# Splitting the first weight load in two, and making the first FFN weights inside the output projection

## The chip, the cores and the metric

The kernel runs on all 8 cores of one Trainium2 chip. Every core runs the same program on its own rows; two cores share a batch entry. The metric is the device time of the slowest core in microseconds, lower is better. Engines: PE (TensorE, with PEld for its weight loads), DVE (VectorE), ACT (ScalarE), POOL (GpSimd) and SP (SyncE). DMAs are issued from the instruction queues of POOL and SP.

## The reference

One transformer layer on x of shape (4, 2048, 2048):

```
q, k, v = x Wq^T, x Wk^T, x Wv^T
mem     = sum over 4 memories of softmax weight * (elu1(q) M_m) / (elu1(q) n_m)
local   = causal attention, 16 heads of 128
x1      = layernorm(x + (g*mem + (1-g)*local) Wo^T)
up      = relu(quant8(x1) ternary(Wup)^T)^2          # Wup: 4096 x 2048
out     = layernorm(x1 + quant8(up) ternary(Wdown)^T)
ternary(w) = clip(round(w / s), -1, 1) * s,   s = mean |w|
```

The ternary weights are found on the chip: a comparison of each weight with +threshold and -threshold.

## The kernel before, in words

Each core takes one batch entry, computes q for all of its 2048 tokens (stage A1), k, v and attention head pair by head pair (A2), and from then on works on its own 1024 tokens: memory retrieval (B0, B1), transposes (B2), output projection with residual (B3), quantisation with the first columns of the FFN's up product (C1), the rest of the up product (C2), then the down product and the second layernorm (C3 to C5).

The order is written out by hand. Each engine has one list of instructions, which it works through strictly in the order of the calls that emitted them; `k.emit(engine, fn, waits, inc)` puts one in, with waits on semaphores ahead of it. A DMA is issued from the list of POOL (`gpsimd`) or SP (`sync`), and its waits hold back everything behind it in that list. `k.ch(sem)` waits until the last DMA on that semaphore has landed.

**Stage A1** (L315). x (64 DMAs in four batches, a batch issued when the one before has landed), the small `mntb` and Wq (`wqb`, one DMA of 2048 x 2048 at L273) are loaded with a cast from f32 to bf16, all on POOL's queue and on the semaphore `gld`. The first group of 16 matmuls (oc = 0, lc = 0, dc = 0 to 15) waits for all of Wq.

**Stage B3** (L942 to L1010). Loop over ht = 0 to 3 (512 output columns each) and ss = 0 to 7 (128 tokens each). For each ht, POOL issues four DMAs into `wos[ht % 2]` (L942), after the matmuls of ht - 2 that read this buffer. For each (ht, ss): SP loads the residual `xos` (L955, two buffers), DVE casts it to `xob` (L963), PE does 16 matmuls (L970, of which the first waits for `wos`) and one more that adds `xob` (L976), ACT evacuates into `x2` (L982) and sums squares (L988), DVE finds minimum and maximum (L992, L996), and for ht = 3 four small reductions (L1001 to L1010). DVE's cast for a pair stands in its list ahead of that pair's reductions and behind those of the pair before.

**Between B3 and C1.** After the loop come `emit_wfs_dma(0)`, `emit_tern_up(0)`, `emit_wfs_dma(1)`, `emit_tern_up(1)` and `emit_wfs_dma(2)`. `emit_wfs_dma(it)` (L1028) loads 256 columns of Wup into the single staging tile `wfs`, half 0 from POOL's list, half 1 from SP's; each half waits until the ternary step of `it - 1` has read it. `emit_tern_up(it)` makes `wub[it % 2]` on DVE with two instructions a half (L1045, L1050). Then come 17 small operations on `sr8`, `sc3`, `ncol`, `f1col` and `cq1` (L1063 to L1097, one square root on ACT), and the loop of C1, which for each ss quantises (ACT L1133, L1138; DVE L1144, L1148), transposes (PE L1157, DVE L1163) and does the up products of it = 0 and 1 (PE L1109).

**Places in SBUF** (bytes of a partition). `lsT`, which B3's matmuls read to their end, is at 98304 to 131072; `wub1` is at 98304, so its ternary step waits for `b3_last`, the last matmul of B3. `wfs` is at 73728, `wub0` at 90112. 65536 to 73728 is free in B3 to C2 but for the tile `tnbg`, which nothing writes.

Of the kernel before, what the change touches and what calls it, by code (L numbers as in the profile page):

```python
# [9 lines left out]
BF16 = mybir.dt.bfloat16  # L10
I32 = mybir.dt.int32
ALU = mybir.AluOpType
# [4 lines left out]
D = 2048  # L17
# [3 lines left out]
NCK = 16  # L21
# [110 lines left out]
def build_program(dbg=False):  # L132
# [4 lines left out]
    wqT = dt("wqT", [D, D], F32, kind="ExternalInput")  # L137
# [5 lines left out]
    wupT = dt("wupT", [D, DI], F32, kind="ExternalInput")  # L143
# [25 lines left out]
    with root:  # L169
        k = K()  # L170
# [5 lines left out]
        gld = mksem("gld")  # L176
        sld = mksem("sld")
        sst = mksem("sst")
        tmm = mksem("tmm")
        vve = mksem("vve")  # L180
# [5 lines left out]
        s_up = mksem("s_up")  # L186
        s_dn = [mksem(f"s_dn{i}") for i in range(2)]
        s_xo = [mksem(f"s_xo{i}") for i in range(2)]
        s_sw = [mksem(f"s_sw{i}") for i in range(2)]
        gcc = mksem("gcc")  # L190
        sdbg = mksem("sdbg")

        ov = Overlay(nc)
# [20 lines left out]
        thrup = P("thrup", 128, 1, F32)  # L214
# [17 lines left out]
        def bank_w(b):  # L232
            return [bank_guard[b]] if bank_guard[b] is not None else []
# [5 lines left out]
        wqb = ov.tensor("wqb", [128, NCK * D], BF16, 0, 1)  # L239
# [5 lines left out]
        xchunk_ld = []  # L245
        for lc in range(4):
            for dc in range(NCK):
# [3 lines left out]
                    waits=k.ch(gld) if dc == 0 else (), inc=gld, inc_k=16)  # L251
            xchunk_ld.append(gld.n)
            k.chend(gld)
        for dst, src in ((biasb, biasc), (idb, identb), (onecb, onescb),
# [7 lines left out]
            waits=k.ch(sld), inc=sld, inc_k=16)  # L262
# [4 lines left out]
            waits=k.ch(gld), inc=gld, inc_k=16)  # L267
        k.chend(gld)
        k.emit("sync", lambda sy: sy.dma_start(gb[0:1, 0:1], gate.ap()),
               waits=k.ch(sld), inc=sld, inc_k=16)  # L270
        k.chend(sld)
        consts_ld = sld.n
        k.emit("gpsimd", lambda g: g.dma_start(  # L273
            wqb[:].rearrange("p (c w) -> p c w", w=D),
            wqT.ap().rearrange("(c p) w -> p c w", p=128)),
            waits=k.ch(gld), inc=gld, inc_k=16)
        wq_ld = gld.n
        k.chend(gld)
# [31 lines left out]
        for oc in range(NCK):  # L310
            for lc in range(4):
                bank = lc
                wts = [(gld, max(wq_ld, xchunk_ld[lc]))] + bank_w(bank)
                for dc in range(NCK):
                    k.emit("tensor", lambda t, oc=oc, lc=lc, dc=dc, bank=bank: t.matmul(  # L315
                        ps[bank][:, 0:CH],
                        wqb[:, dc * D + oc * 128: dc * D + (oc + 1) * 128],
                        xTb[:, dc * S + lc * CH: dc * S + (lc + 1) * CH],
                        start=(dc == 0), stop=(dc == NCK - 1)),
                        waits=wts if dc == 0 else (),  # L320
                        inc=tmm if dc == NCK - 1 else None)
                mmv = tmm.n
                if lc < 2:
                    k.emit("vector", lambda v, oc=oc, lc=lc, bank=bank: v.tensor_copy(
                        qT[:, oc * OWN + lc * CH: oc * OWN + (lc + 1) * CH],
                        ps[bank][:, 0:CH]),
                        waits=[(tmm, mmv), (vve, vve.n)], inc=vve)
                    bank_guard[bank] = (vve, vve.n)
                else:
                    par = lc - 2  # L330
                    k.emit("vector", lambda v, bank=bank, par=par: v.tensor_copy(
                        qPscr[:, par * CH:(par + 1) * CH], ps[bank][:, 0:CH]),
                        waits=[(tmm, mmv), (vve, sigch["v"])], inc=vve)
                    qcp = vve.n
                    bank_guard[bank] = (vve, qcp)
                    k.emit("scalar", lambda s, par=par: s.activation(
                        scrA1[:, par * CH:(par + 1) * CH],
                        qPscr[:, par * CH:(par + 1) * CH], AF.Relu,
                        scale=-1.0),
                        waits=[(vve, qcp), (sse, sigch["exp"])], inc=sse)  # L340
                    k.emit("scalar", lambda s, par=par: s.activation(
                        scrA2[:, par * CH:(par + 1) * CH],
                        scrA1[:, par * CH:(par + 1) * CH], AF.Exp,
                        scale=-1.0), waits=[(sse, sse.n)], inc=sse)
                    sigch["exp"] = sse.n
                    k.emit("vector", lambda v, par=par: v.scalar_tensor_tensor(
                        scrA1[:, par * CH:(par + 1) * CH],
                        qPscr[:, par * CH:(par + 1) * CH],
                        0.0, scrA2[:, par * CH:(par + 1) * CH],
                        ALU.max, ALU.add),  # L350
                        waits=[(sse, sigch["exp"]), (vve, vve.n)], inc=vve)
                    k.emit("vector", lambda v, oc=oc, par=par: v.reduce_sum(
                        sbarP[:, par * NCK + oc: par * NCK + oc + 1],
                        scrA1[:, par * CH:(par + 1) * CH], AX.X),
                        waits=[(vve, vve.n)], inc=vve)
                    sigch["v"] = vve.n
# [15 lines left out]
               waits=k.ch(sld), inc=sld, inc_k=16)  # L372
# [5 lines left out]
               waits=[(sld, consts_ld)], inc=sse)  # L378
        gsig = sse.n
        wts = [(sse, gsig)] + bank_w(2)  # L380
# [4 lines left out]
               waits=[(tmm, tmm.n)], inc=vve)  # L385
# [51 lines left out]
        for hp in range(8):  # L437
# [4 lines left out]
                waits=[(tmm, kw_t)] + k.ch(s_kv), inc=s_kv, inc_k=16)  # L442
# [6 lines left out]
                waits=[(tmm, vw_t)] + k.ch(s_kv), inc=s_kv, inc_k=16)  # L449
            vld = s_kv.n  # L450
            k.chend(s_kv)
            for hip in range(2):
                for st in range(4):
                    bank = (hip * 4 + st) % 2
                    wts = [(s_kv, kld), (gld, wq_ld)] + bank_w(bank)
                    for dc in range(NCK):
# [5 lines left out]
                            waits=wts if dc == 0 else (),  # L462
# [393 lines left out]
        for ss in range(8):  # L856
            for oc in range(NCK):
# [26 lines left out]
        sr8 = ov.tensor("sr8", [128, 48], F32, 0, 11)  # L884
        wfs = ov.tensor("wfs", [128, NCK * 256], F32, 6, 8, at=73728)
        wub = [ov.tensor("wub0", [128, NCK * 256], BF16, 6, 8, at=90112),
               ov.tensor("wub1", [128, NCK * 256], BF16, 6, 8, at=98304)]
        tnb = ov.tensor("tnb", [128, 2048], BF16, 6, 10, at=172032)
        xqT = ov.tensor("xqT", [128, 8 * D], BF16, 7, 8, at=106496)
        xqtile = ov.tensor("xqtile", [128, D], BF16, 7, 8)  # L890
# [14 lines left out]
        rqtile = ov.tensor("rqtile", [128, 2048], BF16, 9, 10)  # L905

        xob = [ov.tensor(f"xob{i}", [128, CH], BF16, 6, 6) for i in range(2)]
        tnbg = ov.tensor("tnbg", [128, 2048], BF16, 6, 6, at=65536)
        mng = ov.tensor("mng", [128, 32], F32, 6, 8)
        mxg = ov.tensor("mxg", [128, 32], F32, 6, 8)  # L910
        cq1 = ov.tensor("cq1", [128, 16], F32, 6, 8)
# [21 lines left out]
        def g_emit(fn, waits=()):  # L933
            k.emit("gpsimd", fn, waits=[(gcc, last_g[0])] + list(waits),
                   inc=gcc)
            last_g[0] = gcc.n
            return gcc.n

        for ht in range(4):
            buf = ht % 2  # L940
# [12 lines left out]
            for ss in range(8):  # L953
# [46 lines left out]
                if ht == 3:  # L1000
# [10 lines left out]
                        sc3[:, ss:ss + 1], mxg[:, ss * 4:(ss + 1) * 4],  # L1011
                        AX.X, ALU.max))
            wo_t[buf] = tmm.n
        b3_last = tmm.n
        b3_sse = last_s[0]

        up_ld = {}
        tern_half = {}
        up_t = [0, 0]
        tern_v = {}  # L1020

        def emit_wfs_dma(it):
            lds = []
            for dh in range(2):
                sem = s_up if dh == 0 else s_sw[0]
                qeng = "gpsimd" if dh == 0 else "sync"
                w0 = [tern_half[(it - 1, dh)]] if it >= 1 else []
                k.emit(qeng, lambda g, it=it, dh=dh: g.dma_start(  # L1028
                    wfs[:, dh * 2048:(dh + 1) * 2048].rearrange(
                        "p (c w) -> p c w", w=256),  # L1030
                    wupT.ap()[dh * 1024:(dh + 1) * 1024,
                              it * 256:(it + 1) * 256].rearrange(
                        "(c p) w -> p c w", p=128)),
                    waits=w0 + k.ch(sem), inc=sem, inc_k=16)
                lds.append((sem, sem.n))
                k.chend(sem)
            up_ld[it] = lds

        def emit_tern_up(it, eng="vector", extra=()):
            buf = it % 2  # L1040
            em = v_emit if eng == "vector" else g_emit
            sem = vve if eng == "vector" else gcc
            tb = tnb if eng == "vector" else tnbg
            for dh in range(2):
                em(lambda v, dh=dh, tb=tb: v.tensor_scalar(  # L1045
                    tb[:, 0:2048], wfs[:, dh * 2048:(dh + 1) * 2048], -1.0,
                    thrup[:, 0:1], ALU.mult, ALU.is_ge),
                    waits=[up_ld[it][dh], (tmm, up_t[buf]),
                           (vve, sw_v)] + list(extra))
                tv = em(lambda v, dh=dh, buf=buf, tb=tb: v.scalar_tensor_tensor(  # L1050
                    wub[buf][:, dh * 2048:(dh + 1) * 2048],
                    wfs[:, dh * 2048:(dh + 1) * 2048], thrup[:, 0:1],
                    tb[:, 0:2048], ALU.is_ge, ALU.subtract))
                tern_half[(it, dh)] = (sem, tv)
            tern_v[it] = (sem, tv)

        emit_wfs_dma(0)
        emit_tern_up(0)
        emit_wfs_dma(1)
        emit_tern_up(1, extra=[(tmm, b3_last)])  # L1060
        emit_wfs_dma(2)

        v_emit(lambda v: v.tensor_single_scalar(  # L1063
            sr8[:, 8:16], sr8[:, 0:8], 1.0 / D, ALU.mult))
# [468 lines left out]
```

How the kernel before makes its waits and increments, by code:

```python
        def g(e, fn=fn, wl=wl, inc=inc, inc_k=inc_k):  # L64
            for (h, v) in wl:
                e.wait_ge(h, v)
            r = fn(e)
            if inc is not None:
                r.then_inc(inc.h, inc_k)
```

## Time and profile before

| what | us |
|---|---|
| median of 3 runs | 3064.46 (3057.01 to 3067.91) |
| the profiled execution's own time | 3062.41 |
| its span on the slowest core (core 3) | 3060.9 |
| spans of the 8 cores | 3029.0 to 3060.9 |
| PE busy | 2268.7 (74%) |
| DVE busy | 1134.9 (37%) |
| ACT busy | 713.9 (23%) |
| PE waits for Wq at the start | 139.9 |
| stage B3, first to last matmul | 2000.5 to 2129.5 |
| stage C1, first transpose to the next ternary step | 2166.0 to 2325.6 |

Times inside the profile count from the start of the span. The span is the slowest core's, and the own time of the same execution is 1.5 us longer.

### The profile page before, as it was taken

The page shows a single profiled execution, that of the slowest core. Times are in us where ns is not written, and L with a number is a line of the kernel's source. Part 1 is how long each engine was busy: PE and PEld are TensorE (multiplying, and loading weights), DVE is VectorE, ACT ScalarE, POOL GpSimd, SP SyncE. Part 2 cuts the span into 40 slices and gives each one's busy share as a digit, 9 for nine tenths or more (in the row PEclk, how much of TensorE's full clock was granted, in tenths as well). Part 3 has the DMA queues.
Part 4 walks back from the last instruction along what each step waited for, and adds up shares of the span by engine and source line. Part 5 has one row for each costly group of instructions (what it writes and reads, how often), then busy time and mean ns, then how long its engine had stood idle before and what let it go on. Part 6 is the DMA issues. An engine that isn't in the chain of part 4 may idle for free.

```text
span 3060.9 us, 37676 instructions; the slowest of 8 cores (3029.0 to 3060.9 us)
## 1 busy us (share of the span) xinstructions
PE 2268.7 (74%) x14858; PEld 1452.9 (47%) x14858; DVE 1134.9 (37%) x1393; ACT 713.9 (23%) x1232; POOL 143.5 (5%) x166
## 2 busy tenths in 40 slices
PE   0199799898988988960799999587347992455883
PEld 0044353452543534510788888233225882344773
DVE  0043303324143243245111111535335765655544
ACT  0021123323323223233011111022232222341221
POOL 4000000000000000001000100000000000000000
PEclk9999899999999999975899999599557996677997
DMA  8700142433343333223676580174102442102422
GB/s 107 114 1 1 37 67 83 83 96 96 69 110 73 79 91 95 63 69 38 73 91 76 67 98 4 18 128 108 50 0 83 150 126 83 55 1 89 129 86 110
DMA packets 190002, 229.53 MB, mean 75 GB/s; under 512 B 10499, under 2 KB 157956, under 8 KB 188804
## 3 DMA queue, kind: packets, MB, share of 16 engines
q0 software_dynamic: 129568, 109.08, 23.1%
q1 hardware_dynamic: 59108, 109.66, 11.6%
q10 hardware_dynamic: 1152, 8.39, 0.7%
q8 instruction: 120, 1.97, 0.3%
q14 instruction: 54, 0.44, 0.1%
HBM read 294.23 MB, written 8.39 MB: 99 GB/s over the span
## 4 chain that ended last, share of the span: by engine, by line
PE 65%; DVE 15%; DMA 6%; another core or an unknown queue 5%; issue 3%; ACT 3%; DVEq 2%; POOL 0%; ACTq 0%; POOLq 0%; SPq 0%
PE ps_all L758 15%; PE ps_all L477 8%; PE ps_all L457 7%; PE ps_all L1109 7%; PE ps_all L315 7%; PE ps_all L1304 5%; PE ps_all L526 4%; PE ps_all L521 3%; PE ps_all L544 2%; PE ps_all L970 2%; DVE wdb L1267 2%; DMA wfd<-wdnT 2%; PE ps_all L420 1%; DMA membuf<-mem 1%
## 5 line engine op out<-in xcount | busy, mean ns | idle before, releaser
L758 PE MATMUL ps_all<-membuf,sigT 128*128 128x256 bf16 x4096 | 448.6, 273 | 41.8 <-DMA membuf<-mem 41.8
L758 PEld LDWEIGHTS ps_all<-membuf,sigT 128*128 128x128 bf16 x4096 | 401.4, 98 | 88.8 <-issue 41.8
L315 PE MATMUL ps_all<-xTb,wqb 128*128 128x512 bf16 x1024 | 223.3, 382 | 139.9 <-DMA wqb<-wqT 139.9
L1304 PE MATMUL ps_all<-wdb,rtq 128*128 128x256 bf16 x2048 | 255.9, 293 | 92.2 <-DVE wdb L1267 53.6
L1304 PEld LDWEIGHTS ps_all<-wdb,rtq 128*128 128x128 bf16 x2048 | 213.6, 105 | 134.4 <-issue 95.9
L1109 PE MATMUL ps_all<-wub,xqT 128*128 128x256 bf16 x2048 | 256.0, 292 | 23.0 <-DVE wub L1050 9.6
L1109 PEld LDWEIGHTS ps_all<-wub,xqT 128*128 128x128 bf16 x2048 | 212.1, 104 | 65.5 <-issue 29.5
L477 PE MATMUL ps_all<-vw,xTb 128*128 128x256 bf16 x2048 | 229.9, 276 | 12.4 <-DVE lsT L429 12.4
L457 PE MATMUL ps_all<-xTb,kw 128*128 128x512 bf16 x1024 | 224.1, 381 | 16.4 <-DMA kw<-wkT 16.4
L315 PEld LDWEIGHTS ps_all<-xTb,wqb 128*128 128x128 bf16 x1024 | 100.6, 98 | 262.1 <-issue 142.8
L477 PEld LDWEIGHTS ps_all<-vw,xTb 128*128 128x128 bf16 x2048 | 202.5, 99 | 43.7 <-issue 18.0
L301 DVE TENSOR_REDUCE swpart<-swst 128x1 f32<-128x1024 f32 x128 | 152.9, 1215 | 159.7 <-DMA swst<-wupT 85.7
L408 DVE RECIPROCAL denr<-ps_all 1x512 f32<-1x512 f32 x32 | 106.8, 3337 | 251.7 <-PE ps_all L526 251.7
L567 ACT ACTIVATE expm<-ps_all,biasb 128x1024 bf16<-128x1024 f32 x128 | 141.1, 1116 | 165.9 <-PE ps_all L544 165.9
L778 DVE SCALAR_TENSOR_TENSOR scrB<-ps_all,coefb,scrB 128x256 f32<-128x256 f32 x64 | 31.0, 484 | 398.6 <-ACT scrB L773 393.0
L457 PEld LDWEIGHTS ps_all<-xTb,kw 128*128 128x128 bf16 x1024 | 100.0, 98 | 142.0 <-issue 24.2
L521 PE MATMUL ps_all<-expm,onecb 128*1 128x512 bf16 x384 | 150.2, 391 | 21.9 <-ACT expm L567 11.2
L526 PE MATMUL ps_all<-expm,vpp 128*128 128x512 bf16 x384 | 154.4, 402 | 0.0
L769 ACT ACTIVATE scrB<-ps_all,coefb 128x256 f32<-128x256 f32 x64 | 30.5, 476 | 445.6 <-PE ps_all L758 445.6
L970 PE MATMUL ps_all<-wos,lsT 128*128 128x512 bf16 x512 | 117.7, 384 | 21.1 <-DMA wos<-woT 21.1
L544 PE MATMUL ps_all<-qT,khh 128*128 128x512 bf16 x384 | 123.4, 409 | 5.6 <-ACT vpp L484 5.6
L1117 ACT ACTIVATE rtq<-ps_all,f1col 128x256 bf16<-128x256 f32 x128 | 60.9, 476 | 269.3 <-PE ps_all L1109 269.3
(160 smaller groups left out, 1920.2 us busy)
## 6 DMA issues: line engine op xcount, KB each, us to landing
swst<-wupT SPq DMA_DIRECT2D x64, 512.0 KB, 4.5
swst<-wdnT SPq DMA_DIRECT2D x64, 512.0 KB, 4.3
membuf<-mem POOLq DMA_DIRECT2D x32, 1024.0 KB, 24.6
wfs<-wupT POOLq DMA_DIRECT2D x16, 1024.0 KB, 6.7
wfs<-wupT SPq DMA_DIRECT2D x16, 1024.0 KB, 6.6
wfd<-wdnT SPq DMA_DIRECT2D x16, 1024.0 KB, 6.6
wfd<-wdnT POOLq DMA_DIRECT2D x16, 1024.0 KB, 6.7
xTb<-xT POOLq DMA_DIRECT2D x64, 128.0 KB, 8.4
```

Source lines behind the costliest of these rows:

```text
L301: k.emit("vector", lambda v, buf=buf, idx=idx: v.reduce_sum(swpart2[:, idx:idx + 1], swst[buf][:], AX.X, apply_absolute_value=True), waits ...
L315: k.emit("tensor", lambda t, oc=oc, lc=lc, dc=dc, bank=bank: t.matmul(ps[bank][:, 0:CH], wqb[:, dc * D + oc * 128: dc * D + (oc + 1) * 128 ...
L457: k.emit("tensor", lambda t, hip=hip, st=st, dc=dc, bank=bank: t.matmul(ps[bank][:, 0:CH], kw[:, dc * 256 + hip * 128: dc * 256 + hip * 12 ...
L477: k.emit("tensor", lambda t, ss=ss, dc=dc, bank=bank: t.matmul(ps[bank][:, 0:256], xTb[:, dc * S + ss * 128: dc * S + (ss + 1) * 128], vw[ ...
L521: k.emit("tensor", lambda t, slot=slot, half=half, first=first, last=last, dnb=dnb: t.matmul(dnb[0:1, 0:CH], onecb[:, 0:1], expm[:, slot * ...
L526: k.emit("tensor", lambda t, hip=hip, pc=pc, kb=kb, slot=slot, half=half, first=first, last=last, pvb=pvb: t.matmul(pvb[:, 0:CH], vpp[:, ( ...
L544: k.emit("tensor", lambda t, hip=hip, h=h, o=o, pc=pc, kb=kb, scb=scb, half=half, diag=diag: t.matmul(psc[scb][:, half * CH:(half + 1) * C ...
L567: k.emit("scalar", lambda s, scb=scb, slot=slot, bi=bi: s.activation(expm[:, slot * 1024:(slot + 1) * 1024], psc[scb][:, 0:1024], AF.Exp, ...
L758: k.emit("tensor", lambda t, ss=ss, m=m, dc=dc, bank=bank, buf=buf: t.matmul(ps[bank][:, 0:256], sigT[:, dc * OWN + ss * 128: dc * OWN + ( ...
L970: k.emit("tensor", lambda t, ss=ss, dc=dc, bank=bank, buf=buf: t.matmul(ps[bank][:, 0:CH], attn_inT[:, dc * OWN + ss * 128: dc * OWN + (ss ...
L1109: k.emit("tensor", lambda t, ss=ss, dc=dc, it=it, bank=bank, buf=buf: t.matmul(ps[bank][:, 0:256], xqT[:, ss * D + dc * 128: ss * D + dc * ...
L1304: k.emit("tensor", lambda t, ss=ss, ic=ic, bank=bank, buf=buf: t.matmul(ps[bank][:, 0:256], rtq[:, qbase(ss) + ic * 128: qbase(ss) + ic * ...
```

## The change

Three edits. The load of Wq becomes two DMAs of 1024 rows each, the second issued when the first has landed; the first group's matmuls start on the first half, and the matmul dc = 8 waits for the second. `wub1` moves to 65536 (the unused `tnbg` goes). The five calls that load and make `wub0` and `wub1` and load the third `wfs` are emitted at the end of ht = 2 of B3 instead of behind the loop, without the wait for `b3_last`; the two functions are defined ahead of the loop, unchanged.

```diff
-            wqb[:].rearrange("p (c w) -> p c w", w=D),
-            wqT.ap().rearrange("(c p) w -> p c w", p=128)),
+            wqb[:, 0:8 * D].rearrange("p (c w) -> p c w", w=D),
+            wqT.ap()[0:1024, :].rearrange("(c p) w -> p c w", p=128)),
+            waits=k.ch(gld), inc=gld, inc_k=16)
+        wq_h0 = gld.n
+        k.chend(gld)
+        k.emit("gpsimd", lambda g: g.dma_start(
+            wqb[:, 8 * D:16 * D].rearrange("p (c w) -> p c w", w=D),
+            wqT.ap()[1024:2048, :].rearrange("(c p) w -> p c w", p=128)),
             waits=k.ch(gld), inc=gld, inc_k=16)
         wq_ld = gld.n
...
-                wts = [(gld, max(wq_ld, xchunk_ld[lc]))] + bank_w(bank)
+                wts = [(gld, max(wq_h0, xchunk_ld[lc]))] + bank_w(bank)
...
-                        waits=wts if dc == 0 else (),
+                        waits=wts if dc == 0
+                        else ([(gld, wq_ld)] if dc == 8 else ()),
...
-               ov.tensor("wub1", [128, NCK * 256], BF16, 6, 8, at=98304)]
+               ov.tensor("wub1", [128, NCK * 256], BF16, 6, 8, at=65536)]
...
-        tnbg = ov.tensor("tnbg", [128, 2048], BF16, 6, 6, at=65536)
...
+        def emit_wfs_dma(it):
+            lds = []
+            for dh in range(2):
+                sem = s_up if dh == 0 else s_sw[0]
+                qeng = "gpsimd" if dh == 0 else "sync"
+                w0 = [tern_half[(it - 1, dh)]] if it >= 1 else []
+                k.emit(qeng, lambda g, it=it, dh=dh: g.dma_start(
...
+                    waits=w0 + k.ch(sem), inc=sem, inc_k=16)
...
+        def emit_tern_up(it, eng="vector", extra=()):
...
+                em(lambda v, dh=dh, tb=tb: v.tensor_scalar(
+                    tb[:, 0:2048], wfs[:, dh * 2048:(dh + 1) * 2048], -1.0,
+                    thrup[:, 0:1], ALU.mult, ALU.is_ge),
+                    waits=[up_ld[it][dh], (tmm, up_t[buf]),
+                           (vve, sw_v)] + list(extra))
+                tv = em(lambda v, dh=dh, buf=buf, tb=tb: v.scalar_tensor_tensor(
...
         for ht in range(4):
...
             wo_t[buf] = tmm.n
+            if ht == 2:
+                emit_wfs_dma(0)
+                emit_tern_up(0)
+                emit_wfs_dma(1)
+                emit_tern_up(1)
+                emit_wfs_dma(2)
         b3_last = tmm.n
         b3_sse = last_s[0]
...
-        emit_wfs_dma(0)
-        emit_tern_up(0)
-        emit_wfs_dma(1)
-        emit_tern_up(1, extra=[(tmm, b3_last)])
-        emit_wfs_dma(2)
```

## Rows read from the trace of the kernel before

**Rows 1.** Cores: span and mean granted TensorE clock, slowest core.
```profile
core 3: 3060.9 us, clock 0.871
```

**Rows 2.** The page: busy time of TensorE, and the chain by engine.
```profile
PE 2268.7 (74%) x14858; PEld 1452.9 (47%) x14858; DVE 1134.9 (37%) x1393; ACT 713.9 (23%) x1232; POOL 143.5 (5%) x166
...
PE 65%; DVE 15%; DMA 6%; another core or an unknown queue 5%; issue 3%; ACT 3%; DVEq 2%; POOL 0%; ACTq 0%; POOLq 0%; SPq 0%
```

**Rows 3.** Timeline: start us, length us, engine, line, operation, [idle before <- releaser].
```profile
84.60 1.15 POOL L273 DMA_DIRECT2D wqb<-wqT  x1 [3.87 <-DMA mntb<-mnT]
...
139.86 40.31 PE L315 MATMUL ps_all<-xTb,wqb 128*128 128x512 bf16 x176 [139.86 <-DMA wqb<-wqT]
```

**Rows 4.** Windows: busy us per engine (PE to POOL), clock, DMA share, GB/s.
```profile
84.00:88.00 4.00, 0.00 (x0) 0.00 (x0) 0.00 (x0) 0.00 (x0) 1.15 (x1) 1.00 0.06 8
...
136.00:140.00 4.00, 0.14 (x1) 0.14 (x2) 0.00 (x0) 0.00 (x0) 0.00 (x0) 1.00 0.62 124
```

**Rows 5.** DMA issues: count, KB each, median us to landing.
```profile
wqb<-wqT POOLq DMA_DIRECT2D x1, 8192.0 KB, 55.1
...
mntb<-mnT POOLq DMA_DIRECT2D x1, 16.0 KB, 4.5
```

**Rows 6.** Timeline of DMA issues on GpSimd, stages B3 and C1.
```profile
2063.28 2.97 POOL L942 DMA_DIRECT2D wos<-woT  x4 [27.75 <-PE ps_all L976]
2066.20 0.95 POOL L1028 DMA_DIRECT2D wfs<-wupT  x1
...
2151.09 1.32 POOL L1028 DMA_DIRECT2D wfs<-wupT  x1 [12.07 <-DVE wub L1050]
```

**Rows 7.** Timeline of TensorE, stages B3 and C1.
```profile
2000.45 5.62 PE L970 MATMUL ps_all<-wos,lsT 128*128 128x512 bf16 x16 [21.15 <-DMA wos<-woT]
...
2074.11 0.38 PE L976 MATMUL ps_all<-xob,idb 128*128 128x512 bf16 x1 [0.64 <-DVE xob L963]
...
2092.66 3.62 PE L970 MATMUL ps_all<-wos,lsT 128*128 128x512 bf16 x16
...
2129.12 0.38 PE L976 MATMUL ps_all<-xob,idb 128*128 128x512 bf16 x1 [0.84 <-DVE xob L963]
...
2172.72 3.57 PE L1109 MATMUL ps_all<-wub,xqT 128*128 128x256 bf16 x16 [1.05 <-DVE xqT L1163]
```

**Rows 8.** Timeline of VectorE, end of ht = 2 and end of B3.
```profile
2094.51 0.69 DVE L996 TENSOR_REDUCE mxg<-x 128x1 f32<-128x512 bf16 x1
2095.43 0.43 DVE L963 CAST xob<-xos 128x512 bf16<-128x512 f32 x1 [0.24 <-DVE mxg L996]
...
2133.34 1.28 DVE L1045 TENSOR_SCALAR tnb<-wfs,thrup 128x2048 bf16<-128x2048 f32 x1 [0.18 <-DVE sc L1010]
...
2146.74 1.28 DVE L1045 TENSOR_SCALAR tnb<-wfs,thrup 128x2048 bf16<-128x2048 f32 x1 [5.74 <-DMA wfs<-wupT]
...
2154.50 0.17 DVE L1063 TENSOR_SCALAR sr<-sr 128x8 f32<-128x8 f32 x1
```

**Rows 9.** Tile wos: issue to landing, loads of ht=3, then ht=0.
```profile
DMA to landing us min/median/max: 7.5/11.5/15.2
...
DMA to landing us min/median/max: 9.1/14.4/17.7
```

**Rows 10.** Loads xos (all 32), and one wfs of C1 alone: us to landing.
```profile
DMA to landing us min/median/max: 2.8/3.9/8.0
...
wfs<-wupT POOLq DMA_DIRECT2D x1, 1024.0 KB, 6.6
```

**Rows 11.** Windows after the end of B3: columns as in rows 4.
```profile
2129.60:2131.00 1.40, 0.00 (x0) 0.00 (x0) 0.62 (x1) 1.31 (x4) 0.00 (x0) 0.94 0.00 0
2131.00:2132.00 1.00, 0.00 (x0) 0.00 (x0) 0.75 (x2) 0.10 (x2) 0.00 (x0) 0.50 0.00 0
...
2166.00:2320.00 154.00, 68.56 (x364) 45.25 (x365) 47.83 (x46) 41.48 (x42) 0.00 (x0) 0.53 0.00 0
...
2340.00:2360.00 20.00, 20.00 (x186) 17.92 (x184) 14.25 (x12) 5.60 (x12) 2.64 (x2) 1.00 0.49 155
```

More of the change, by code:

```diff
@@ L937, in g_emit @@
             return gcc.n
+        up_ld = {}
+        tern_half = {}
+        up_t = [0, 0]
+        tern_v = {}
+        def emit_wfs_dma(it):
[5 more added lines that the diff above has]
+                k.emit(qeng, lambda g, it=it, dh=dh: g.dma_start(
+                    wfs[:, dh * 2048:(dh + 1) * 2048].rearrange(
+                        "p (c w) -> p c w", w=256),
+                    wupT.ap()[dh * 1024:(dh + 1) * 1024,
+                              it * 256:(it + 1) * 256].rearrange(
+                        "(c p) w -> p c w", p=128)),
+                    waits=w0 + k.ch(sem), inc=sem, inc_k=16)
+                lds.append((sem, sem.n))
+                k.chend(sem)
+            up_ld[it] = lds
+        def emit_tern_up(it, eng="vector", extra=()):
+            buf = it % 2
+            em = v_emit if eng == "vector" else g_emit
+            sem = vve if eng == "vector" else gcc
+            tb = tnb if eng == "vector" else tnbg
+            for dh in range(2):
+                em(lambda v, dh=dh, tb=tb: v.tensor_scalar(
[4 more added lines that the diff above has]
+                tv = em(lambda v, dh=dh, buf=buf, tb=tb: v.scalar_tensor_tensor(
+                    wub[buf][:, dh * 2048:(dh + 1) * 2048],
+                    wfs[:, dh * 2048:(dh + 1) * 2048], thrup[:, 0:1],
+                    tb[:, 0:2048], ALU.is_ge, ALU.subtract))
+                tern_half[(it, dh)] = (sem, tv)
+            tern_v[it] = (sem, tv)
         for ht in range(4):
@@ L1013, in build_program @@
             wo_t[buf] = tmm.n
+            if ht == 2:
[4 more added lines that the diff above has]
+                emit_wfs_dma(2)
         b3_last = tmm.n
         b3_sse = last_s[0]
[L1017 to L1055, printed above, removed]
-        emit_wfs_dma(0)
-        emit_tern_up(0)
-        emit_wfs_dma(1)
-        emit_tern_up(1, extra=[(tmm, b3_last)])
-        emit_wfs_dma(2)
         v_emit(lambda v: v.tensor_single_scalar(
```

## The prediction

> **What bounds the kernel now.** I read the cores first, to know whose page this is: core 3, the slowest [rows 1]. TensorE is busy for 74% of the span and makes 65% of the chain that ended last [rows 2]. So an edit counts only where TensorE stands still, and I went to the two places that the diff touches, with the timeline of each engine. At the start TensorE waits 139.86 us, in the end for Wq [rows 3]. Between B3 and C1 it waits too: the last matmul of B3 starts at 2129.12 [rows 7], DVE is done with B3's reductions just ahead of 2133.34, then makes the two ternary tiles until 2154.50, and only then starts the small operations that C1 needs [rows 8]. In B3 itself TensorE runs nearly without a gap until ht = 3, where 36.9 us pass from 2092.66 to 2129.5 [rows 7].
>
> **Part 1, the ternary work leaves the end of B3.** The block is 2154.50 - 2133.34 = 21.2 us of DVE alone, with TensorE idle all along and the small operations queued behind it [rows 8]. Nothing else is late there: those operations need B3's reductions only. So this stretch gains **21.2 us**. The wait for `b3_last` costs nothing now, as DVE comes to it later than that matmul, and its going gains nothing.
>
> **Part 2, the same block arrives behind ht = 2.** In DVE's list it stands between the last reduction of (2,7), at 2094.51 for 0.69 us, and the cast of (3,0), now at 2095.43 [rows 8]. It starts at 2095.38, that is 37.96 us earlier than before, and keeps its inner shape: half 0 of the first tile, then POOL can load half 0 of the second `wfs`, DVE sits idle 5.74 us for it [rows 8], and goes on. The first `wfs` is there in time: POOL issues half 0 right behind the `wos` of ht = 2, SP half 1 behind the last `xos` of ht = 2. The cast of (3,0) and what hangs on it waits for the block, and this alone gives back those 21 us, for TensorE halts at its matmul L976.
>
> **Part 3, what is queued behind the waits on POOL and SP.** Before, POOL issued the four `wos` loads of ht = 3 at 2063.28, when the matmuls of ht = 1 had ended, 29.4 us ahead of their use at 2092.66, and the `wfs` load behind them [rows 6, 7]. Now they stand behind three `wfs` loads. The third waits until DVE has read half 0 of the second tile: in the block of before it was issued at 2151.09, which is 17.75 us after the start, and took 1.32 us [rows 6, 8]. So the first `wos` load of ht = 3 is issued at 2095.38 + 17.75 + 1.32 = 2114.45. How long does it take? From the first issue (2063.28) to the last landing it took 2.2 us to the fourth issue (three quarters of the 2.97) and 15.2 to its landing, 17.4 us; the set of ht = 0, with another four behind it on the queue, took 2.2 + 17.7 = 19.9 [rows 6, 9]. The new one has the third `wfs` half just ahead on its queue and the other half beside it on SP's (each 6.6 us to landing with little else under way [rows 10]), but only two `xos` loads beside it instead of four or five. I add 3.1 us to 17.4 and take **20.5** (an estimate; the bounds are 17.4, nothing added, and 19.9 + 6.6 = 26.5, the longest load and all of a `wfs` on top). TensorE starts ht = 3 at 2135.0 instead of 2092.66: **+42.3**. On SP the `xos` of (3,0) waits for the third `wfs` too, until about 2117, and lands within 2.8 to 8.0 us [rows 10]: 2125 at the latest, hidden under `wos`, as is the cast. If `wos` came at once, this would hold TensorE.
>
> The Trainium skill (DMA: Bandwidth & Descriptors, Specifications and Anatomy of one DMA) gives a core about 358 GB/s from HBM and some 2 us fixed for a DMA; four reads of 1 MiB are then 13.7 us, and by it the total below would be about 7 us smaller. The rows have 17.4, and all eight cores load at once, so I go by the rows.
>
> **Part 4, the clock.** Behind B3's end the granted clock is 0.94 over the first 1.4 us and 0.50 (1.2 GHz) in the next [rows 11]. So the new gap of some 40 us ends at the low level, and the first group of ht = 3 goes as that of ht = 0 did after its wait: 16 matmuls in 5.62 us against 3.62 [rows 7]. The rest of ht = 3 is paced by DVE's reductions, not by TensorE (36.9 us for 8 groups against 8 x 3.62 = 29), so the delay passes through: **+2.0**. C1 stays as it is: TensorE's gap ahead of it shrinks from 36 to 15 us, far beyond the 1.4 us in which the clock fell, and it has 0.53 there in any case [rows 11].
>
> **Part 5, small things in B3.** The `wos` load of ht = 3 no longer competes with the `xos` of ht = 2; that had cost TensorE 0.64 us [rows 7]. **-0.6**. The first `wfs` half moves beside the `wos` load of ht = 2, behind it on the same queue; I cost it at nothing, for the `wos` has 27 us of matmuls as cover, and the same pair stood together before.
>
> **Part 6, Wq in halves.** One DMA took 55.1 us [rows 5]. Of this hardly anything moves in the first 3.4 us (share 0.06 to 88.00), and 0.62 of the last window says that data ended about 138.5, 1.3 us ahead of the matmul [rows 3, 4]. The second half is issued only when the first has landed, so this 4.7 us is paid again; the 16 KB `mntb` takes 4.5 us to landing with next to no data, which says the same [rows 5]. Between the two I take **+4.6**: the second half lands at 144.4. In return 8 matmuls of the first group are done by about 114: 8 x 0.226 us (3.62 / 16 [rows 7]) = **-1.8**. No more, since TensorE works in order and each group needs all 16. The gap in between leaves the clock low at the restart, as it was before. Together **+2.8**. Bounds: -1.8, if the other cores' pauses let the second half run that much faster, and +4.0, if POOL's 1.15 us for the issue [rows 3] comes on top of the 4.6.
>
> By the Trainium skill's 2 us fixed a DMA (same page, Anatomy of one DMA) the split would cost 2.0 - 1.8 = 0.2 instead of 2.8. The rows show more than twice that overhead, so I stay with them.
>
> **The move of `wub1`** changes no duration; C1 and C2 read and write it as before, and nothing else is at 65536 until C2 is over.
>
> **Sum.** -21.2 + 42.3 + 2.0 - 0.6 + 2.8 = +25.3 us. Against its own time of 3062.4 that is 3087.7; the median of the runs is 2.1 us above that execution, so **3090 us**. Where the second `wfs` lands sooner than here, the block is shorter at both places, and the difference stays: another core as the slowest one doesn't change the sum.
>
> **Rivals.**
> *Only DVE's order counts (no change).* If `wos` of ht = 3 were in place by the time of the cast (2116.6), the block would merely be moved: +21.2 - 21.2, with 2.0 for the clock, -0.6 and +2.8: +4.2, 3069 us. For that it would have to land 2.2 us after its issue; the quickest single load of these took 7.5 [rows 9]. Against it speaks the order of POOL's list. 5%.
> *The clock pays (not slower).* If the short gap left TensorE at the high level through C1, its 16 groups there would take 16 x 0.1075 = 1.72 us (186 matmuls in 20.00 [rows 11]) instead of 3.57 [rows 7]: 16 x 1.85 = 29.6 saved, total -4.3, 3060 us. It decides if the clock holds over 15 us of idleness; the row shows it gone after 1.4 [rows 11]. With some other gain that I don't see: 4%.
> *A longer load.* With `wos` at 26.5 and the split at +4.0 it is 25.3 + 6.0 + 1.2 = +32.5, 3097 us, and more if the `xos` come late as well. 13%.
> *A cheap one.* `wos` at 17.4, the split at -1.8 and C1 3 us shorter by a clock a little above its 0.53: 25.3 - 3.1 - 4.6 - 3 = +14.6, 3079 us. 10%.
> *The split does what it promises.* TensorE does start some 26 us earlier, but gains 1.8; it is in the forecast.
>
> **The numbers.** The forecast (3080 to 3098) has 68%. A measurement of this kernel tells from no change about 0.3%, 9.2 us: only a result under 3073.7 would not be slower. Faster 4%, same 5%, slower 91%. The range, 3075 to 3104, takes in the cheap case and most of the long one.
>
> **What will show it.** In the trace after: TensorE starts near 114 us with 8 matmuls and waits again until about 144; POOL issues the `wos` of ht = 3 about 22 us after the end of ht = 2, and TensorE waits some 42 us for it, with the first group at the low clock; behind B3's end the small operations follow the reductions at once, 15 us before C1's first transpose. I am wrong if the gap behind ht = 2 is near 20 us, if the wait for `wos` is not what ends it, or if C1 is shorter than the 160 us of before by more than 5.

## The result and the profile after

The changed kernel is **slower by 0.73%** (ratio to the kernel before 1.0073, 95% interval 1.0058 to 1.0088), that is 22 us (18 to 27). Its median is 3090.8 us over all runs, with 3067.6 for the kernel before over as many; in some executions the cores of one die run at a lower granted clock and take longer, and the ratio leaves these out. The forecast was 3090 against 3064.5, +25.3 us by its sum, slower with a chance of 91%.

The slowest core of the kernel after, of which the page is (core: span, mean granted clock):

```profile
core 5: 3087.4 us, clock 0.869
```

The page's busy time and the chain by engine, which answer to [rows 2]:

```profile
PE 2271.7 (74%) x14858; PEld 1453.7 (47%) x14858; DVE 1135.0 (37%) x1393; ACT 711.6 (23%) x1232; POOL 144.1 (5%) x167
...
PE 66%; DVE 15%; DMA 10%; issue 3%; ACT 3%; DVEq 1%; POOL 1%; ACTq 0%; POOLq 0%; SPq 0%
```

TensorE is as busy as before: its work has not grown, its waits have. The 10% of DMA in the chain can't be set against the 6% of before, as the start, which was "another core or an unknown queue" with 5% before, is now counted with it; the timelines have to tell. The timeline of GpSimd's DMA issues and of TensorE at the start, beside [rows 3]:

```profile
84.01 0.88 POOL L273 DMA_DIRECT2D wqb<-wqT  x1 [3.23 <-DMA mntb<-mnT]
113.14 0.88 POOL L279 DMA_DIRECT2D wqb<-wqT  x1 [28.25 <-DMA wqb<-wqT]
```

```profile
112.75 3.57 PE L321 MATMUL ps_all<-xTb,wqb 128*128 128x512 bf16 x8 [112.75 <-DMA wqb<-wqT]
141.42 38.87 PE L321 MATMUL ps_all<-xTb,wqb 128*128 128x512 bf16 x171 [25.10 <-DMA wqb<-wqT]
```

TensorE begins 27 us sooner, does eight matmuls, and stands still for 25.10 us again. These eight take 3.57 us, 0.45 us each, twice the 0.23 of a matmul at the full clock (3.62 / 16 [rows 7]); the windows have no clock record yet so early in the run and show 1.00, so here the durations tell the level. The same two engines in B3, beside [rows 6, 7]:

```profile
2032.87 2.96 POOL L990 DMA_DIRECT2D wos<-woT  x4 [46.47 <-PE ps_all L1024]
2035.79 0.94 POOL L956 DMA_DIRECT2D wfs<-wupT  x1
2098.35 1.12 POOL L956 DMA_DIRECT2D wfs<-wupT  x1 [61.62 <-DVE wub L978]
2112.49 1.31 POOL L956 DMA_DIRECT2D wfs<-wupT  x1 [13.02 <-DVE wub L978]
2113.79 3.01 POOL L990 DMA_DIRECT2D wos<-woT  x4
```

```profile
2090.87 0.38 PE L1024 MATMUL ps_all<-xob,idb 128*128 128x512 bf16 x1
2135.83 4.91 PE L1018 MATMUL ps_all<-wos,lsT 128*128 128x512 bf16 x16 [44.58 <-DMA wos<-woT]
...
2173.56 0.38 PE L1024 MATMUL ps_all<-xob,idb 128*128 128x512 bf16 x1 [1.19 <-DVE xob L1011]
2189.06 1.01 PE L1165 MATMUL ps_all<-idb,xqtile 128*128 128x128 bf16 x8 [15.12 <-DVE xqtile L1156]
```

The four `wos` loads of ht = 3 are now issued at 2113.79, 23 us after the end of ht = 2 (the matmul at 2090.87) and behind a `wfs` load that waited 13.02 us for DVE. TensorE waits 44.58 us for them. Behind the end of B3 its gap is 15.12 us, where it was 36.5. DVE's timeline, beside [rows 8]:

```profile
2093.78 1.29 DVE L973 TENSOR_SCALAR tnb<-wfs,thrup 128x2048 bf16<-128x2048 f32 x1 [0.18 <-DVE mxg L1044]
...
2108.12 1.29 DVE L973 TENSOR_SCALAR tnb<-wfs,thrup 128x2048 bf16<-128x2048 f32 x1 [6.67 <-DMA wfs<-wupT]
...
2113.43 2.35 DVE L978 SCALAR_TENSOR_TENSOR wub<-wfs,thrup,tnb 128x2048 bf16<-128x2048 f32 x1
2132.17 0.43 DVE L1011 CAST xob<-xos 128x512 bf16<-128x512 f32 x1 [16.39 <-DMA xos<-x_own]
...
2177.25 0.16 DVE L1058 TENSOR_REDUCE sc<-mxg 128x1 f32<-128x4 f32 x1
2177.52 0.17 DVE L1071 TENSOR_SCALAR sr<-sr 128x8 f32<-128x8 f32 x1
```

The block stands behind ht = 2 in its old shape, idle for 6.67 us in the middle. At 2132.17 the cast of (3,0) had waited for the residual, not for the block. Behind B3 the last reduction, at 2177.25, is followed at 2177.52 by the small operations, as forecast. The landing times of the four `wos` loads of ht = 3, and of the two `xos` loads issued behind the third `wfs` on SP:

```profile
DMA to landing us min/median/max: 9.9/15.5/19.6
```

```profile
DMA to landing us min/median/max: 15.6/15.9/16.3
```

And the window of C1, beside [rows 11] (busy time of PE, PEld, DVE, ACT, POOL, then clock, DMA share, GB/s):

```profile
2189.00:2346.00 157.00, 70.86 (x382) 46.62 (x383) 47.84 (x46) 41.81 (x43) 0.00 (x0) 0.57 0.00 0
```

C1 has 0.57 of the full clock against 0.53, and in the mean over the cores it is 0.56 in both kernels: it stays at the low level most of the time.

Averages over the eight cores of each kernel's profiled execution, from the same kinds of rows: B3 from the start of its first matmul to the start of its last, and from there to the first small operation (a ratio is of all timed runs that count, not of this one execution).

| kernel | B3 us | to the small operations us | sum us | ratio to before |
|---|---|---|---|---|
| before | 129.0 | 23.8 | 152.7 | |
| after | 171.8 | 4.0 | 175.8 | 1.0073 |
| e2, moved only | 171.7 | 4.0 | 175.7 | 1.0080 |
| e3, wos ahead | 157.2 | 4.0 | 161.2 | no interval |
| e11, wos and xos ahead | 150.6 | 4.0 | 154.5 | 1.0000 |
| e6, cast ahead | 119.4 | 23.3 | 142.7 | 0.9975 |
| e7, spread | 137.2 | 4.3 | 141.5 | 0.9959 |
| e9, spread earlier | 123.5 | 3.9 | 127.4 | 0.9927 |

B3 grows by 42.8 us and 19.8 are won back: +23.1, which lies within the interval of the measured difference. Of the 42.8, the gap behind ht = 2 adds 42.2 and ht = 3 after it 2.3 (38.7 us against 36.4), while ht = 0 to 2 take 1.7 less (90.6 against 92.3). The way from Wq's first issue to the start of A1's last matmul is 275.8 us before and 275.6 after.

### The profile page after: what moved, and what is told of

The parts are those of the page before. It is cut to its first block, busy times and chain, and to the rows that moved or that the text cites. A ratio compares the mean times of both kernels' runs of the same rounds, so it can differ in the third digit from the quotient of the medians.

```text
span 3087.4 us, 37677 instructions; the slowest of 8 cores (3051.9 to 3087.4 us)
## 1 busy us (share of the span) xinstructions
PE 2271.7 (74%) x14858; PEld 1453.7 (47%) x14858; DVE 1135.0 (37%) x1393; ACT 711.6 (23%) x1232; POOL 144.1 (5%) x167
## 4 chain that ended last, share of the span: by engine, by line
PE 66%; DVE 15%; DMA 10%; issue 3%; ACT 3%; DVEq 1%; POOL 1%; ACTq 0%; POOLq 0%; SPq 0%
PE ps_all L765 15%; PE ps_all L1117 8%; PE ps_all L484 7%; PE ps_all L464 7%; PE ps_all L321 7%; PE ps_all L1312 5%; PE ps_all L533 3%; PE ps_all L528 3%; PE ps_all L1018 3%; PE ps_all L551 2%; DMA wqb<-wqT 2%; DVE wdb L1275 2%; DMA wfd<-wdnT 2%; DMA xTb<-xT 1%; PE ps_all L427 1%
```

## The experiments

**e1, the split of Wq alone.** The kernel before with the first edit of the change only:

```diff
+            wqb[:, 0:8 * D].rearrange("p (c w) -> p c w", w=D),
+            wqT.ap()[0:1024, :].rearrange("(c p) w -> p c w", p=128)),
...
+            wqb[:, 8 * D:16 * D].rearrange("p (c w) -> p c w", w=D),
+            wqT.ap()[1024:2048, :].rearrange("(c p) w -> p c w", p=128)),
...
-                        waits=wts if dc == 0 else (),
+                        waits=wts if dc == 0
+                        else ([(gld, wq_ld)] if dc == 8 else ()),
```

> The kernel before with the split of Wq alone (two row halves). The prediction's theory: a pause of 4.6 us is paid a second time and 8 matmuls are gained, +2.8 us in all, TensorE starting near 113 us and again near 144. The rival, for which the changed kernel's trace speaks (28.7 and 28.3 us for the halves against 53 to 55 us for the whole): the pause is largely made up, because the eight cores share what the others leave, and the edit is worth -1 to +1 us.

Measured: ratio 1.0000 (0.9986 to 1.0015). In the mean over the cores, TensorE starts on the last piece 54.8 us after the first issue (54.3 in the changed kernel) against 52.9 before, and A1's last matmul starts 275.9 us after it against 275.8. The edit costs nothing and gains nothing that can be measured. All the traces with the old Wq load or the two halves say the same: 51.9 to 53.2 us in the five kernels with one DMA (before, e2, e6, e7, e9), 54.3 to 54.8 in the four with two halves (after, e1, e3, e11). A pause costs 1.9 us by their means, not 4.6, and the eight matmuls pay for it.

**e4, four row pieces.** The suspected cost three times over:

```diff
+        for wi4 in range(4):
+            k.emit("gpsimd", lambda g, wi4=wi4: g.dma_start(
+                wqb[:, wi4 * 4 * D:(wi4 + 1) * 4 * D].rearrange(
...
+                wqT.ap()[wi4 * 512:(wi4 + 1) * 512, :].rearrange(
...
+                        else ([(gld, wq_q[dc // 4])] if dc % 4 == 0 else ()),
```

> The kernel before with Wq in four DMAs of 512 rows, each issued when the one before has landed, and the first group's matmuls waiting quarter by quarter. The prediction's theory, with its suspected cost three times over: 3 x 4.6 - 12 x 0.226 = +11 us, the last quarter landing some 14 us later after the issue than the single DMA. The rival (the pauses are made up by the sharing among cores): -3 to +3 us.

Measured: ratio 1.0020 (1.0010 to 1.0031), +6 us (3 to 9.5). The timeline of TensorE on the slowest core shows the four starts:

```profile
101.44 1.87 PE L320 MATMUL ps_all<-xTb,wqb 128*128 128x512 bf16 x4 [101.44 <-DMA wqb<-wqT]
117.43 1.87 PE L320 MATMUL ps_all<-xTb,wqb 128*128 128x512 bf16 x4 [14.12 <-DMA wqb<-wqT]
132.62 1.86 PE L320 MATMUL ps_all<-xTb,wqb 128*128 128x512 bf16 x4 [13.32 <-DMA wqb<-wqT]
147.10 33.07 PE L320 MATMUL ps_all<-xTb,wqb 128*128 128x512 bf16 x143 [12.61 <-DMA wqb<-wqT]
```

Each quarter lets four matmuls run and TensorE waits 12.6 to 14.1 us more. The last quarter is used 58.3 us after the first issue in the mean (52.9 before), so a pause costs (58.3 - 52.9) / 3 = 1.8 us, the same as in e1; three of them less twelve matmuls are 5.4 - 2.7 = 2.7 us, and A1 does end 2.7 us later. The result lies between the two forecasts, 11 and at most 3. The price from the landings holds for both kernels; of the +6 only these 2.7 us are placed, and where the rest is stays open.

**e2, the move alone.** The changed kernel with Wq in one DMA:

```diff
-            wqb[:, 0:8 * D].rearrange("p (c w) -> p c w", w=D),
-            wqT.ap()[0:1024, :].rearrange("(c p) w -> p c w", p=128)),
...
+            wqb[:].rearrange("p (c w) -> p c w", w=D),
+            wqT.ap().rearrange("(c p) w -> p c w", p=128)),
```

> The changed kernel with Wq loaded in one DMA again: only the ternary block and its loads are moved. The prediction's theory: +22.5 us (-21.2 + 42.3 + 2.0 - 0.6) against the kernel before, the gap behind ht = 2 41 to 45 us. If the rival on the split holds, this is all of the +23 us measured, and e1 is nothing.

Measured: ratio 1.0080 (1.0063 to 1.0097), +25 us. TensorE waits 40.2 to 45.2 us for `wos` of ht = 3 on the eight cores. The moved block is the whole of the result.

**e3, the `wos` loads of ht = 3 first.** One step of the cause taken away, the order of GpSimd's list:

```diff
             if ht == 2:
+                emit_wos(3)
                 emit_wfs_dma(0)
...
+            if ht < 3:
+                emit_wos(ht)
```

> The changed kernel with the four wos loads of ht = 3 emitted ahead of the wfs loads on GpSimd's list; everything else as in the changed kernel. The theory that the waits in GpSimd's list are the cause: the loads go out at the end of ht = 1 again, TensorE does the 16 matmuls of (3,0) at once and halts only at the one that adds the residual, until DVE has done the block (21.1 us) and the xos load, which SP issues behind the third wfs, has landed (about 4 us more): 25.6 + 2.0 - 21.2, about +6 us against before. The rival that DVE's block alone makes the stall: no gain over the changed kernel, +23 us.

Measured: its four timed runs are too few for an interval (the lowest is 3061.4 us), so this verdict is the trace's: +8.5 us by the sums in the table, near the forecast of +6 and far from the rival's +23. GpSimd's issue of the loads, SP's issues, and TensorE:

```profile
2067.18 2.96 POOL L992 DMA_DIRECT2D wos<-woT  x4 [26.66 <-PE ps_all L1032]
...
2116.49 1.32 POOL L956 DMA_DIRECT2D wfs<-wupT  x1 [11.98 <-DVE wub L978]
```

```profile
2089.00 31.29 SPq L956 DMA_DIRECT2D wfs<-wupT  x3
2120.39 32.23 SPq L1011 DMA_DIRECT2D xos<-x_own  x8
```

```profile
2127.36 0.58 PE L1032 MATMUL ps_all<-xob,idb 128*128 128x512 bf16 x1 [27.61 <-DVE xob L1019]
```

The loads go out at 2067.18 again, when ht = 1 is done, and no matmul waits for them. TensorE halts at the one that adds the residual, for 27.61 us here and 25.4 to 27.6 on the cores; B3 takes 157.2 us instead of 171.8. So 14.6 of the 42.8 us are GpSimd's list (16.6 in ht = 3, less 2.0 in ht = 0 to 2, where the `wos` loads are again beside the `xos`). The row of SP names the next wait: its `xos` loads for ht = 3 start at 2120.39, behind three `wfs` loads. The first of them lands 6.8 us after its issue in the mean over the cores (6.2 to 8.0), where it took 15.1 in the changed kernel (14.0 to 17.1) with the four `wos` loads beside it.

**e11, the `xos` loads first as well.** On top of e3:

```diff
                 emit_wos(3)
+                emit_xos(3, 0)
+                emit_xos(3, 1)
                 emit_wfs_dma(0)
```

> e3 with the two xos loads of (3,0) and (3,1) issued ahead of the wfs loads on SP as well, so that of the changed kernel's move only DVE's own order is left. Theory: the stall behind ht = 2 falls from the 25.4 to 27.6 us of e3 to that of the block, 21 us or a little less, and what the block costs there is what its going from the end of B3 gains: -19.8 + 19 to 21 + 2.0, +1 to +4 us against before. Rival: xos isn't what e3 waited for, its gap of 26 us stays, +8.

Measured: ratio 1.0000 (0.9972 to 1.0028). SP's and TensorE's timelines, slowest core:

```profile
2072.43 23.90 SPq L993 DMA_DIRECT2D xos<-x_own  x7
2096.43 22.11 SPq L956 DMA_DIRECT2D wfs<-wupT  x3
```

```profile
2118.85 0.59 PE L1042 MATMUL ps_all<-xob,idb 128*128 128x512 bf16 x1 [18.89 <-DVE xob L1029]
```

The gap is 18.89 us here, 18.9 to 20.6 on the cores, and B3 150.6 us: another 6.6 us were SP's list. The runs alone don't separate the forecast (+1 to +4) from the rival (+8), as their interval is 9 us to either side; the gap does, and the table has +1.8. The three parts are what each step took away in this order. What is left, 21.6 us over the 129.0, is DVE's block with the slow first group behind it, and it is what its going from the end of B3 gives back (19.8), within 2 us.

**e5, Wq by columns.** The kernel before, four DMAs again, but each with all rows of 512 columns:

```diff
+        for wc in range(4):
+            k.emit("gpsimd", lambda g, wc=wc: g.dma_start(
+                wqb[:].rearrange("p (c w) -> p c w", w=D)[
+                    :, :, wc * 512:(wc + 1) * 512],
+                wqT.ap()[:, wc * 512:(wc + 1) * 512].rearrange(
...
-                wts = [(gld, max(wq_ld, xchunk_ld[lc]))] + bank_w(bank)
+                wts = [(gld, max(wq_q[oc // 4], xchunk_ld[lc]))] + bank_w(bank)
```

> The kernel before with Wq in four DMAs of 512 output columns each (all 2048 rows), oc = 0 to 3 waiting for the first only. If the split by rows is worth nothing because every group of matmuls needs all rows, this one lets 256 matmuls (55 us at the full clock) run on the first quarter: TensorE starts once, near 102 us instead of 140, and doesn't stop again, since a quarter lands some 17 us after its issue: -35 to -38 us. Rival: the pieces of 2 KB are loaded so much more slowly, or the loads and the matmuls are held up by each other, that less than 15 us are left.

Measured: ratio 0.9864 (0.9846 to 0.9882), -42 us. GpSimd and TensorE on the slowest core:

```profile
87.81 1.15 POOL L275 DMA_DIRECT2D wqb<-wqT  x1 [5.80 <-DMA mntb<-mnT]
103.15 1.14 POOL L275 DMA_DIRECT2D wqb<-wqT  x1 [14.19 <-DMA wqb<-wqT]
...
134.92 1.14 POOL L275 DMA_DIRECT2D wqb<-wqT  x1 [14.23 <-DMA wqb<-wqT]
```

```profile
102.76 223.31 PE L320 MATMUL ps_all<-xTb,wqb 128*128 128x512 bf16 x1024 [102.76 <-DMA wqb<-wqT]
```

TensorE starts 37 us before it did and does all 1024 matmuls of the stage in one stretch of 223.31 us; the quarters are issued 15 to 16 us after one another, but TensorE needs a new one only every 56 us (223.31 / 4), so nobody waits for their pauses. A1 is 38.4 us shorter by the traces; the runs' gain is 4 us above the forecast's upper end of 38, which lies within the interval (36 to 47).

**e6, the cast one pair ahead.** The kernel before, the cast and its `xos` load of the next pair emitted ahead of this pair's reductions:

```diff
-                xcv = v_emit(lambda v, xb=xb: v.tensor_copy(
+                xcv = xcv_of[ht * 8 + ss]
...
+                emit_xos_cast(ht * 8 + ss + 1)
                 v_emit(lambda v, ss=ss, ht=ht: v.tensor_reduce(
```

> The kernel before with each residual cast (and its xos load) of B3 emitted one pair earlier on DVE, ahead of the reductions of the pair whose matmuls just ended. Theory that in ht = 3 TensorE is paced by the cast standing behind the reductions (4.66 us a pair against 3.67): ht = 3 takes 29.5 instead of 36.9 us, and the 0.6 to 1.0 us stalls for xos stay: -7 us. Rival: the reductions are the pace whatever their order, 0.

Measured: ratio 0.9975 (0.9952 to 0.9998), -8 us (0.6 to 15). The last group of B3 on TensorE:

```profile
2114.44 3.62 PE L982 MATMUL ps_all<-wos,lsT 128*128 128x512 bf16 x16
2117.89 0.38 PE L988 MATMUL ps_all<-xob,idb 128*128 128x512 bf16 x1
```

The groups of ht = 3 follow each other at 3.67 us, where they took 4.66 before; ht = 3 takes 29.1 us instead of 36.4, and B3 is 119.4 us (129.0). It was the cast's place in DVE's list that paced ht = 3; the small stalls for `xos` are gone too.

**e7, the block in pieces.** The cast of e6, `wub1` at its new place, the block in eight instructions behind the reductions of single pairs of ht = 1 and 2, `wos` loads two ht ahead:

```diff
+            (1, 0): [lambda: emit_wfs_half(0, 0), lambda: emit_wfs_half(0, 1)],
+            (1, 5): [lambda: tern_ts(0, 0)],
+            (1, 6): [lambda: tern_stt(0, 0), lambda: emit_wfs_half(1, 0)],
...
+            (2, 1): [lambda: emit_wfs_half(1, 1), lambda: tern_ts(1, 0)],
...
+            (2, 6): [lambda: tern_stt(1, 1)],
```

> The same cast order, and the ternary block cut into its eight DVE instructions, one behind the reductions of a pair in ht = 1 and 2, with each wfs load emitted where what it waits for is done, and the wos loads two ht ahead of their use. Theory: the block fits into DVE's idle time in B3 if no list is blocked: TensorE has no gap over 2 us in B3 after the first wos, the 21 us behind B3 are gone: -21 - 7 = -28 us. Rival: DMA in ht = 1 and 2 (wos, wfs, xos together) is too much, and wos of ht = 2 or 3 comes late by 5 to 10 us: -18 to -23.

Measured: ratio 0.9959 (0.9942 to 0.9977), -13 us: a miss, as even the rival had -18. SP and TensorE on the slowest core, and SP's issues of the stretch from 2075.3 with their time to landing:

```profile
2075.06 0.38 SPq L947 DMA_DIRECT2D wfs<-wupT  x1
2075.54 26.54 SPq L1002 DMA_DIRECT2D xos<-x_own  x6
```

```profile
2091.93 0.59 PE L1052 MATMUL ps_all<-xob,idb 128*128 128x512 bf16 x1 [12.35 <-DVE xob L1010]
```

```profile
xos<-x_own SPq DMA_DIRECT2D x1, 256.0 KB, 15.7
```

One `xos` load, issued at 2075.54 behind a `wfs` load that had waited on SP for DVE, took 15.7 us to land beside it and beside four `wos` loads (3.9 is the median before [rows 10]), and TensorE stood still for 12.35 us, 10 to 13 on every core. The rival had named the wrong load: not `wos` came late but the small one.

**e9, the pieces earlier.** The first `wfs` in the middle of ht = 0, the second load of SP six pairs into ht = 1:

```diff
+            (0, 3): [lambda: emit_wfs_half(0, 0, [(tmm, tmm.n)]),
+                     lambda: emit_wfs_half(0, 1)],
+            (0, 6): [lambda: tern_ts(0, 0)],
...
+            (1, 5): [lambda: emit_wfs_half(1, 1)],
```

> e7 with the same pieces some ten pairs earlier: the first wfs loaded in the middle of ht = 0, when no wos is under way, the second on GpSimd behind the wos loads of ht = 2 and on SP six pairs into ht = 1, after what it waits for is long done. In e7 TensorE stood still 10 to 13 us for one xos load, issued behind a wfs load that waited on SP, together with four wos loads. If that was where its missing 15 us went: no gap over 3 us, B3 in 120 to 122 us on every core (129 before), -27 to -30 us against before. Rival: the sum of DMA in ht = 1 and 2 is what stalls it, wherever it stands: -15 us again.

Measured: ratio 0.9927 (0.9889 to 0.9965), -22 us (11 to 34). The waits of TensorE in B3 on the slowest core (total, times, longest):

```profile
PE ps_all L1048 <- DMA wos<-woT: 21.3, 1, 21.3
PE ps_all L1054 <- DVE xob L1012: 4.8, 3, 4.3
```

The 12 us stall has shrunk to 4.3 here and to between 0.5 and 4.0 on the others. B3 is 123.5 us (forecast 120 to 122), and the stage with what follows 25 us shorter than before. The interval alone holds the rival's -15 too; it is the stall's going that decides. Where the missing 15 us of e7 went is settled as to its place; the rest of the stalls is still the `xos` load.

**e8 and e10, both places together.** e7 and e9, each with the columns of e5.

> e7 with the Wq load by columns of e5. The two places have nothing in common, so the gains add: about -64 us (2%). Rival: less than the sum of e5 and e7 by over 8 us, for instance because a core that starts earlier meets the others' loads differently.

> e9 with the Wq load by columns. Gains of e5 (-42) and e9 add: -69 to -72 us, 2.3%. If e9 is no better than e7: -54 us.

Measured: e8 0.9829 (0.9802 to 0.9856), -52 us; e10 0.9822 (0.9795 to 0.9849), -55 us (46 to 63). e8 falls short of its forecast of -64, which counted on -28 of e7; with e7's own 12.6 and e5's 41.7 the sum is 54, near the measured 52. e10 is below its forecast of 69 to 72; e5 and e9 as measured sum to 64, just outside its interval, though e9's own is 11 us to either side. In the profiled execution of e10 the slowest core takes 2998.3 us, and in the mean over the cores A1 is 37.7 us shorter than before and B3 takes 123.2 us, so the two parts are both there; why the runs show less than their sum stays open. e10 is not shown to be faster than e8. Both beat either kernel by 1.7% and more.

## Why the prediction was right

**Part 1** (the block leaves the end of B3, -21.2). Right; 19.8 in the mean over the cores. The 21.2 was core 3's own, one of the two cores (0 is the other) where DVE sat idle longest for the second `wfs`: 5.7 and 5.8 us, against 3.2 to 4.2 on the rest.

**Parts 2 and 3** (the delay behind ht = 2, +42.3). Right in size, 40.0 to 44.6 us with a mean of 42.1, and in cause: e3 and e11 take B3's 42.8 us apart into 14.6 of GpSimd's list, 6.6 of SP's and 21.6 of DVE's own. The load of `wos` took 22.0 us on core 5 (2113.79 to 2135.83) where 20.5 was taken from bounds of 17.4 and 26.5. One sentence in it was wrong: the `xos` of (3,0) would be there by 2125. It was issued at 2116.4 and took about 16 us, to 2132, twice the 8.0 that was the longest before; `wos` hid it by 3 us only. By e3 it was the four `wos` loads beside it that made it so long. The same wait for a residual load later cost e7 half of its gain.

**Part 4** (the clock, +2.0). The first group took 4.9 to 6.4 us on the cores, 5.9 in the mean, against 3.62: +2.3. The delay passed through, but not for the reason given: e6 shows that DVE's reductions don't pace ht = 3, the place of the cast behind them does. C1 kept the low level behind the 15 us gap, and took 157.9 us instead of 157.2 in the mean, from its first transpose to the next ternary step.

**Part 5** (-0.6). Right in direction, a size too small: ht = 0 to 2 take 90.6 us in the mean, in e2 too, against 92.3 before. Where the `wos` loads of ht = 3 stand beside the `xos` again, the 1.7 us are lost again (92.6 in e3, 93.0 in e11).

**Part 6** (the split, +2.8). Wrong in size: 0.0 by e1, -0.2 by the traces. The failed term is "this 4.7 us is paid again": the pause on one core is nearly as long as that, but the last landing comes only some 1.9 us later. Windows of the changed kernel (columns as above), of core 5 between its halves, of core 7, whose pause lies in the window, and of core 6, which is still loading its first half:

```profile
112.00:116.00 4.00, 3.25 (x8) 1.02 (x8) 0.00 (x0) 0.00 (x0) 0.88 (x1) 1.00 0.01 1
...
100.00:110.00 10.00, 3.57 (x8) 1.04 (x8) 0.00 (x0) 0.00 (x0) 0.88 (x1) 1.00 0.67 102
...
100.00:110.00 10.00, 0.00 (x0) 0.00 (x0) 0.00 (x0) 0.00 (x0) 0.00 (x0) 1.00 1.05 199
```

On core 5 next to nothing moves for 4 us. From 100 to 110 us the cores 0, 2 and 7, which pause in it, move 102 to 108 GB/s, and the cores 1, 3, 5 and 6, which don't, 178 to 207; before, all eight have 155 to 168 there. That is what cores would show that share the memory and use what the others' pauses leave, the lower bound that the prediction named. No run had a core alone, and each core's times count from its own start, so the cause is likely and only the price is shown. The price is near the 2 us fixed cost that the Trainium skill (DMA: Bandwidth & Descriptors, Anatomy of one DMA) gives for a DMA, which the prediction had weighed and set aside. As the pause on the core is 4 us all the same, the agreement here is one of numbers and may be luck.

**The sum** (+25.3) came out at +23.1 by the traces and 22 by the runs. The terms were off by +1.4 (part 1), about 0 (parts 2 and 3), +0.3 (part 4), -1.1 (part 5) and -2.8 (part 6); that they nearly cancel is in part luck, but the large terms and their cause were right. None of the three signs of being wrong appeared: the gap was 42 us, `wos` ended it, and C1 was not shorter. Of the rivals, *only DVE's order counts* was tried by e11: with both lists cleared the change is worth nothing, as that rival said of its case, but the changed kernel isn't that case. *The clock pays* didn't happen.

## What to carry to other kernels

Work that leaves a waiting place has to arrive in a place where its engine is idle and no list is held up: here it went from one stretch without cover to another, and the DMAs that stood behind its loads' waits cost as much again. For each wait that is moved, look down every issuing engine's list for the next transfer that somebody needs. And cut a weight load so that a whole group of first results needs one piece only: four pieces by columns gave 42 us, four by rows cost 6, and two by rows gave 0.

## What the runs showed of the hardware

Two things were unexpected. An extra, serial DMA in a stage where all eight cores load at once cost some 1.9 us of the stage's loading time, not the 4.6 that its idle edges add up to (e1, e4). And a 256 KB load from SP's queue, 3.9 us in the median of B3 before, took 15.6 to 16.3 us when four cast loads of GpSimd and a 1 MB load ahead of it on its own queue were under way (after, and 15.7 in e7), so that the smallest transfer was one of the last to arrive. Behind the 1 MB load alone it took 6.8 us in the mean (e3).
